# Own-key probabilities transposed and copied first, and multiplied at full height against a zero-padded tile

## What is computed

```python
x = x + (x @ W0[id] + b0[id])                       # expert chosen per batch
x = x + (x @ W1.T + scaling * (x @ A.T) @ Bm.T)     # adapter chosen per batch
x = x + attention(x)                                # below
x = x + (w3[subject].T @ x + b3[subject])           # mixes the 64 tokens
```

## Time and profile before

| | |
|---|---|
| median of 3 runs | 975.33 us (974.92 to 979.87) |
| the profiled execution, own time | 973.05 us |
| its span, first to last instruction | 970.5 us |
| mean granted TensorE clock | 0.991 of full speed |
| PE (matmul) busy | 935.1 us, 96% |
| VectorE, ScalarE, POOL busy | 604.6, 383.8, 513.4 us |

### The profile page before, as it was taken

How to read it: one execution, slowest core, us unless ns; L and a number is a source line. 1 busy time by engine, 2 the same in 40 slices (tenths; PEclk the granted TensorE clock), 3 DMA queues, 4 the chain that set the end, 5 groups by cost and what they waited for, 6 DMA issues and landing times.

```text
span 970.5 us, 22302 instructions
## 1 busy us (share of the span) xinstructions
PE 935.1 (96%) x6253; PEld 690.1 (71%) x6253; DVE 604.6 (62%) x1788; ACT 383.8 (40%) x1061; POOL 513.4 (53%) x469
## 2 busy tenths in 40 slices
PE   6899999999999999999996899999999999999998
PEld 4566766667666676676765677778778788787785
DVE  6434344657566554446643677777777787777875
ACT  2121221212212122121213556566565665666653
POOL 1255464454644558745366566555665555555530
PEclk9999999999999999999998999999999999999999
DMA  9789888686786776867645565665666666666641
GB/s 305 267 278 306 276 304 277 211 271 224 253 280 220 258 247 229 279 229 253 231 141 164 150 195 176 194 207 175 197 184 192 209 204 198 181 195 210 206 136 45
DMA packets 105162, 212.48 MB, mean 219 GB/s; under 512 B 29563, under 2 KB 52056, under 8 KB 96930
## 3 DMA queue, kind: packets, MB, share of 16 engines
q1 hardware_dynamic: 71042, 145.54, 44.4%
q0 software_dynamic: 25088, 57.74, 20.0%
q10 hardware_dynamic: 8992, 8.73, 2.8%
HBM read 204.39 MB, written 33.86 MB: 245 GB/s over the span
## 4 chain that ended last, share of the span: by engine, by line
PE 92%; DMA 2%; issue 2%; DVE 1%; ACT 1%; POOL 1%; SPq 1%; DVEq 0%; POOLq 0%; ACTq 0%
PE banks L587 11%; PE banks L802 9%; PE banks L705 9%; PE banks L753 9%; PE banks L790 7%; PE banks L626 6%; PE banks L634 6%; PE banks L636 6%; PE banks L771 6%; PE banks L730 4%; PE banks L795 4%; PE banks L695 3%; PE banks L838 3%; PE banks L710 3%; PE banks L597 2%
## 5 line engine op out<-in xcount | busy, mean ns | idle before, releaser
L546 POOL DMA_INDIRECT ring<-new_rows,idx x128 | 130.0, 1016 | 84.1 <-DVE big L1272 54.8
L458 POOL TENSOR_TENSOR rms<-ss,neg_half 128x12 f32<-128x12 f32 x31 | 70.8, 2285 | 175.5 <-DVE ss L1181 175.5
L930 ACT ACTIVATE big<-big,neg_max 128x320 f32<-128x320 f32 x256 | 141.3, 554 | 2.7 <-DVE neg_max L1236 2.5
L1236 DVE CUSTOM_DVE_ANT_0 big<-banks,mask 128x320 f32<-128x320 f32 x256 | 114.7, 486 | 36.0 <-PE banks L753 33.2
L587 PE MATMUL banks<-ring 128*64 128x512 f32 x512 | 117.1, 599 | 2.7 <-DMA ring<-in_w 2.7
L871 ACT ACTIVATE x2t_hi<-banks 128x512 fp32r<-128x512 f32 x32 | 19.1, 597 | 235.2 <-PE banks L597 235.2
L920 ACT ACTIVATE kt<-banks 128x384 f32<-128x384 f32 x128 | 62.1, 485 | 100.7 <-PE banks L731 100.7
L753 PE MATMUL banks<-kt,q_in 64*128 64x128 f32 (+2 forms) x768 | 89.0, 365 | 3.1 <-ACT kt L920 3.1
L587 PEld LDWEIGHTS banks<-ring 128*64 128x64 f32 x512 | 34.1, 136 | 81.0 <-issue 79.9
L535 POOL DMA_INDIRECT ring<-new_rows,idx x64 | 61.5, 961 | 55.1 <-PE banks L777 51.2
L1272 DVE TENSOR_SCALAR big<-big,recip 128x320 f32<-128x320 f32 x256 | 86.0, 398 | 2.3
(11 more groups left out here) (169 smaller groups left out, 1982.8 us busy)
## 6 DMA issues: line engine op xcount, KB each, us to landing
ring<-in_w SPq DMA_DIRECT2D x62, 1024.0 KB, 6.0
ring<-in_xt SPq DMA_DIRECT2D x32, 256.0 KB, 2.7
x_in<-in_x SPq DMA_DIRECT2D x32, 256.0 KB, 5.6
bias_in<-in_b SPq DMA_DIRECT2D x64, 128.0 KB, 5.4
x_dram<-x SPq DMA_DIRECT2D x32, 256.0 KB, 5.0
q_dram<-q_t ACTq DMA_DIRECT2D x32, 256.0 KB, 2.3
new_rows<-kv_out SPq DMA_DIRECT2D x32, 256.0 KB, 4.8
q_in<-q_dram SPq DMA_DIRECT2D x64, 128.0 KB
```

The lines of the kernel that those rows point to most:

```text
L546: pool.indirect_dma_start(out=kv[:, s, c, :], out_offset=None, in_=new_rows, in_offset=bass.IndirectOffsetOnAxis(ap=idx[:, b, 1 + c:2 + c] ...
L930: nc.scalar.activation(prob[:, s % 2, g * NK:(g + 1) * NK], sm[:, s % 2, g, :], ACT.Exp, bias=neg_max[:, s % 2, g:g + 1], scale=-1.0, accu ...
L1236: V.tensor_tensor_reduce(sm[:, s % 2, g, :], ps_s[g], mask[:, s % 2, k0:k0 + NK], 1.0, 3.0e38, ALU.add, ALU.min, accum_out=neg_max[:, s % ...
```

## The change

`pt2` becomes four times [128 x 128]: for each q, a tile with its own 64 partitions filled and the other 64 zero. GpSimd zeroes it once at the start. The own transposes move ahead of the eight others and now follow a wait for all four groups (before, the first four transposes waited for two groups and the next four for all). `copy_own` moves ahead of `copy_second`, is split in two instructions of 64 partitions by 256 columns, and waits once for the zeroing. The own products read all 128 partitions.

```diff
+        pt2 = sb("pt2", [P, 2, GP, P])
...
-        pt2 = sb("pt2", [P, 2, P])
...
             nc.gpsimd.memset(neg_half[:, :], -0.5).then_inc(pool_set, 1)
+            nc.gpsimd.memset(pt2[:, :, :, :], 0.0).then_inc(pt2_set, 1)
...
                 def transpose_probs():
 
+                    pe.wait_ge(prob_ready, G * b)
+                    wait(pe, pt2_ready, b - 1)
+                    wait(pe, ot_ready, b - 1)
+                    for p in range(GP):
+                        last = nc.tensor.transpose(ps_pt2[:, p * P:(p + 1) * P], prob[:, r % 2, (5 * p + 2) * P:(5 * p + 3) * P], ident[:, :])
+                    last.then_inc(pt_done, 1)
                     for p, copied in ((0, pt0_ready), (1, pt1_ready)):
-                        pe.wait_ge(prob_ready, G * b - G + 2 * p + 2)
                         wait(pe, copied, b - 1)
...
-                    wait(pe, pt2_ready, b - 1)
-                    wait(pe, ot_ready, b - 1)
-                    for p in range(GP):
-                        last = nc.tensor.transpose(ps_pt2[:, p * P:(p + 1) * P], prob[:, r % 2, (5 * p + 2) * P:(5 * p + 3) * P], ident[:, :])
-                    last.then_inc(pt_done, 1)
...
-                            last = nc.tensor.matmul(ps_o[HD * q:HD * q + HD, p * P:(p + 1) * P], kv[T * q:T * q + T, r, 2, v0:v0 + HD],
-                                                    pt2[T * q:T * q + T, p, :], start=False, stop=(p == GP - 1), skip_group_check=True)
+                            last = nc.tensor.matmul(ps_o[HD * q:HD * q + HD, p * P:(p + 1) * P], kv[:, r, 2, v0:v0 + HD],
+                                                    pt2[:, q, p, :], start=False, stop=(p == GP - 1), skip_group_check=True)
...
                 def copy_second():
 
-                    act.wait_ge(pt_done, 3 * b - 1)
+                    act.wait_ge(pt_done, 3 * b)
...
                 def copy_own():
 
-                    act.wait_ge(pt_done, 3 * b)
-                    nc.scalar.activation(pt2[:, :, :].rearrange("p q t -> p (q t)"), ps_pt2[:, 0:GP * P], ACT.Copy).then_inc(pt2_ready, 1)
+                    if isinstance(b, int) and b == 1:
+                        act.wait_ge(pt2_set, 1)
+                    act.wait_ge(pt_done, 3 * b - 2)
+                    for q in range(2):
+                        last = nc.scalar.activation(pt2[T * q:T * q + T, q, :, :].rearrange("p g t -> p (g t)"), ps_pt2[T * q:T * q + T, 0:GP * P],
+                                                    ACT.Copy)
+                    last.then_inc(pt2_ready, 1)
...
                 if on(b, 1, NB):
+                    copy_own()
                     copy_second()
-                    copy_own()
...
-                    dve.wait_ge(pt_done, 3 * b - 2)
+                    dve.wait_ge(pt_done, 3 * b - 1)
```

More of the change, by code:

```diff
@@ L213, in build @@
         s_shared, s_done, kt_done, pt_done, pv_done = sem("s_shared"), sem("s_done"), sem("kt_done"), sem("pt_done"), sem("pv_done")
-        wo_done, l3_done = sem("wo_done"), sem("l3_done")
+        wo_done, l3_done, pt2_set = sem("wo_done"), sem("l3_done"), sem("pt2_set")
         ld_mask = sem("ld_mask")
```

## The result

The changed kernel takes 985.63 us (median of 4 runs, 984.32 to 988.03) against 975.12 us of the kernel before: ratio 1.0128, 95% interval 1.0098 to 1.0158. It is **slower by 1.3%**, 0.6 us above the predicted range.

A forecast was written before the change was run, and what follows sets the result against it. TensorE, busy 96% of the span, was taken as the bound, with even turns' value products already waiting for ScalarE. +2.4 us for 30 pairs and +0.3 at each stage end gave +3, about 978.3 us; range 969 to 985.

The forecast's parts named there:

- TensorE's gain: Own products at full height in stage two: one of two changes of form disappears, saving 0.16 us a batch, 10 us for 64.
- what ScalarE pays: Own copy on ScalarE: one copy of 256 columns becomes two, adding 0.27 us in every turn.
- The even turn: Stage two, batches whose value products already wait for ScalarE's copies: +0.27 + 0.04 - 0.16 = +0.15 us (+0.11 to +0.22).
- The odd turn: Stage two, alternate batches: second key copy ends 0.16 us later against 0.23 slack, so the turn changes by -0.07 (0 to -0.16).
- a pair above 13.7: Sign in the later profile: two successive stage-two turns above 13.7 us would mean ScalarE's delay also comes round through VectorE.
- my sum: Stage two: +0.08 us per two turns (-0.05 to +0.22), +2.4 for 30 pairs; with the stage's ends +3 us.
- The slower rival: ScalarE's delay reaches TensorE in both turns, through the odd turn's second key copy: 9 us, about 984 us; chance 0.17.
- The unsaved change of form: Gap before own products belongs to something else and stays: a pair loses 0.31 to 0.35 us, about 986 us; chance 0.10.
- likeliest case: Whole kernel: time within about 0.5% of before, edges 970.5 and 980.2 us; chance 0.56.

## Why the prediction was wrong

**TensorE's gain: right.** -0.16 a batch; measured 0.15 a turn, in both turns with a whole copy and in the even turn with half copies. The gap before the own products belonged to the change of form, and the scores kept theirs. By the rule on draining in "TensorEngine Tiling (Array Packing)" of the Trainium skill, the trace agrees. The rule on weight loads and row groups in Part 3 of the page "TensorE: Matmul & The Clock Gate" of the Trainium skill does not describe this: eight loads of full height took 0.50 us, beside running products of full height, where the measurement decides.

**The failed step: "what ScalarE pays".** I took +0.27 us a turn for the second copy and gave 0.13 and 0.37 as ends. It was 0.77 - 0.27 = **+0.50**, outside both ends. The 0.27 was right for the instruction; missing were two changes of first partition at about 0.12 each. I had noted that no row shows a 64-partition instruction on ScalarE, and yet bounded only its own length, not its effect on the start of the next. Nor did the two ends go into the range of the sum, which keeps the half copy at 0.27 throughout.

**The even turn.** Predicted +0.15, measured 7.53 - 7.23 = +0.30. By my steps with the right price it would be 0.50 + 0.04 - 0.16 = +0.38. The traces give four parts, medians of the steady turns counted from the scores. The first copy starts at 4.60 and not 4.52 (+0.08, mostly the exponentials, which wait 0.06 longer for VectorE's maximum). The copies take 1.38 to the last one's end and not 0.85 (+0.53: the 0.50, and `copy_second` itself 0.60 and not 0.57). The load follows `copy_second` by 0.07 (709.63 + 0.60 = 710.23 to 710.30), where I had put 0.22 + 0.04 (-0.15 against the kernel before). The products save 0.15. Together +0.31. That the even turn's products already waited for ScalarE is shown: a whole copy in the new order, with no more work for ScalarE, lets them start 0.15 sooner. I had said 0.1. The own transposes being early did buy nothing: the first copy starts 4.52 after the scores in either order. What the new order gained with a whole copy came from the distance behind the last copy, which I had made longer, not shorter.

**The odd turn.** Predicted -0.07, measured 6.32 - 6.20 = +0.12. The delay of the second key copy was 0.41 and not 0.16 (5.80 us after the scores, 717.59 - 711.79, before 714.06 - 708.67 = 5.39), since 0.50 and not 0.27 went in and about 0.1 was swallowed, as predicted. The slack was 0.29, as the load needs 0.05 and not 0.11 behind the copy: 0.41 - 0.29 = 0.12.

**The way round through VectorE** stood in the prediction only as a sign, "a pair above 13.7". The pair took 13.86, and the chain shows that way; my sum had nothing for it. Its size in the even turn is the 0.06 by which the exponentials start later.

**Errors that offset each other.** The kernel with both halves at partitions 0 to 63 has the price I had assumed, 0.26 a copy, and all else as in the changed kernel. A pair took 7.26 + 6.06 = 13.32 us, 0.11 less than before, where my sum had 0.08 more. So with its price right my forecast would have been too slow by 0.19 a pair, some 6 us, mainly for the 0.26 that I had put behind `copy_second`. The changes of first partition, four in a pair of turns, cost 13.86 - 13.32 = 0.54 a pair, some 16 us. That the miss was only 7 us (978.3 against 985.63) is luck.

**The sum and the rivals.** +0.42 a pair for 30 pairs is 12.6 us; the scores of all 64 batches took 11.9 us longer from first to last, the span 12. The slower rival, ScalarE's delay in both turns, named the place and the size (984 us) and had 0.17; its half copy of 0.30 was passed. Its own reason was wrong, a wait of 0.11 behind the key copy (it was 0.05), and that its time comes so near is chance in part. The unsaved change of form, 986 us by its sum, would have been hard to tell by the time alone; the form in the trace excludes it. The forecast had the right sign (+0.3%), but its likeliest case was no change, with a chance of 0.32 for slower.

## What to carry to other kernels

When an instruction is split into two on part of the partitions, count its columns and also each change of the first partition between neighbours on ScalarE; and where no row shows the form, let the upper end include its neighbours. When an engine is within 0.1 to 0.3 us of the bound, as ScalarE was here, a gain on the bound and a cost on the neighbour don't add up: follow the chain around a whole pair of turns, through every engine that waits for the late one. If zeros are needed so that a product can be of full height, the operand that is prepared off the path is the place for them; here that gained 0.8% on one occasion and lost 0.4% on another, and stage one paid some 4 to 5 us for it.

## What was not expected of the hardware

On ScalarE a change of first partition (0 to 64 or back) delays the next start by 0.11 to 0.14 us, while 64 partitions after 128 with the same first one start no later; a scale read from a column makes a copy of 256 columns about 0.09 us longer. The load that waits for a last copy of 512 columns started 0.07 us after its end, behind a last `copy_own` of 256 columns 0.22. And TensorE can stand still for about 0.9 us behind the even turn's products at a granted clock of 1.00, on some occasions and not on others: with two single turns that were 4.2 and 2.5 us longer, this made stage two of the kernel before 32 us longer.
